# The deep stage's band mask: from TensorE's products to an addition on VectorE

## The reference

```
bq, bk2 = windows of 32 queries, each with the 64 keys of the window before and its own
mask = (it < jb) | (it > jb + w) | (jb == -1)
sim  = einsum('bhwie,bhwje->bhwij', bq, bk2) * 8
sim  = where(mask, -max, sim)
attn = softmax(sim, -1)
out  = einsum('bhwij,bhwje->bhwie', attn, bv2)
```

## Time and profile before

| | us |
|---|---|
| median of 3 runs | 4492.48 (4480.17 to 4496.16) |
| the profiled execution | 4489.61 |
| its span in the trace | 4487.9 |

### The profile page before, as it was taken

The page is one execution under the profiler, slowest core; times in us unless marked ns, Lnnn a source line. Parts: engine busy times, 40 slices in busy tenths (PEclk is TensorE's granted clock), DMA queues, the critical chain, the costliest instruction groups (busy, mean ns, idle before and its releaser), DMA issues.

```text
span 4487.9 us, 148433 instructions
## 1 busy us (share of the span) xinstructions
PE 4237.0 (94%) x66604; PEld 2403.9 (54%) x66604; DVE 3256.5 (73%) x4169; ACT 2676.0 (60%) x3161; POOL 2128.2 (47%) x1151
## 2 busy tenths in 40 slices
PE   7998899867999999999999996799999999999998
PEld 4544433434555555555555553455555555555554
DVE  6566666565877877877877866677877877877874
ACT  1451355323776776776776762466766766766764
POOL 0110000013665665666665650566666666666663
PEclk8998899978999999999999997899999999999999
DMA  2000000001111211121121111111211211121111
GB/s 84 1 2 1 0 1 1 1 0 35 33 33 29 58 33 54 33 58 30 33 58 29 33 33 50 24 31 31 58 32 31 58 32 55 33 57 30 33 33 29
DMA packets 78612, 144.88 MB, mean 32 GB/s; under 512 B 18648, under 2 KB 24992, under 8 KB 76448
## 3 DMA queue, kind: packets, MB, share of 16 engines
q1 hardware_dynamic: 77984, 135.39, 11.7%
HBM read 39.91 MB, written 1.05 MB: 9 GB/s over the span
## 4 chain that ended last, share of the span: by engine, by line
PE 77%; POOL 8%; issue 7%; DVE 6%; ACT 2%; DMA 0%; SPq 0%; POOLq 0%; DVEq 0%; ACTq 0%
PE psum L1307 13%; PE psum L1359 7%; PE psum L1332 6%; PE psum L1320 6%; PE psum L1276 5%; PE psum L667 5%; PE psum L1378 5%; PE psum L1290 4%; POOL arena L1739 3%; PE psum L1408 3%; PE psum L1424 3%; PE psum L1418 3%; PE psum L1373 3%; PE psum L699 3%; PE psum L721 3%
## 5 line engine op out<-in xcount | busy, mean ns | idle before, releaser
L1739 POOL TENSOR_TENSOR arena<-arena 128x1024 f32<-128x1024 f32 x384 | 722.3, 1902 | 881.8 <-ACT arena L1487 881.8
L1733 POOL TENSOR_TENSOR arena<-arena 128x1024 f32<-128x1024 f32 x384 | 907.5, 2363 | 245.0 <-DVE arena L1608 245.0
L1604 DVE TENSOR_TENSOR arena<-psum,arena 128x1024 f32<-128x1024 f32 x384 | 467.6, 1218 | 616.8 <-ACT arena L1480 616.6
L1480 ACT ACTIVATE arena<-psum 128x1024 f32<-128x1024 f32 x384 | 392.4, 1022 | 288.2 <-PE psum L1307 288.2
L1359 PEld LDWEIGHTS psum<-arena 64*64 64x64 f32 x24576 | 395.6, 135 | 211.8 <-issue 211.8
L1493 ACT ACTIVATE arena<-psum 128x1024 f32<-128x1024 f32 x384 | 390.8, 1018 | 194.6 <-PE psum L1320 194.6
L1608 DVE TENSOR_TENSOR arena<-psum,arena 128x1024 f32<-128x1024 f32 x384 | 466.4, 1215 | 0.0
L1615 DVE TENSOR_REDUCE h_pair<-arena 128x16 f32<-128x1024 f32 x384 | 464.2, 1209 | 0.0
L1359 PE MATMUL psum<-arena 64*64 64x32 f32 x24576 | 437.9, 221 | 5.2 <-DVE arena L1582 5.1
L1320 PE MATMUL psum<-w_ident,arena 128*128 128x128 f32 x3072 | 416.3, 279 | 23.5 <-POOL arena L1739 15.1
L1320 PEld LDWEIGHTS psum<-w_ident,arena 128*128 128x128 f32 x3072 | 338.2, 141 | 162.0 <-POOL arena L1739 94.6
(11 more groups left out here) (266 smaller groups left out, 7087.0 us busy)
## 6 DMA issues: line engine op xcount, KB each, us to landing
arena<-arena SPq DMA_DIRECT2D x672, 128.0 KB, 2.4
deep_wqkv<-in_deep_wqkv SPq DMA_DIRECT2D x6, 1536.0 KB, 7.2
arena<-in_deep_wqkv SPq DMA_DIRECT2D x6, 1536.0 KB, 7.1
arena<-arena SPq DMA_DIRECT2D x96, 64.0 KB, 2.0
deep_wo<-in_deep_wo SPq DMA_DIRECT2D x6, 512.0 KB, 7.5
arena<-in_deep_wo SPq DMA_DIRECT2D x6, 512.0 KB, 7.5
deep_w<-in_deep_w SPq DMA_DIRECT2D x6, 341.0 KB, 7.6
arena<-in_deep_w SPq DMA_DIRECT2D x6, 341.0 KB, 7.6
```

Source lines behind the costliest of these rows:

```text
L1480: nc.scalar.activation(qk_sq[:, HALVES[half], :], qk_half, ACT.Square).then_inc(de.deep_qk_squared, 1)
L1604: nc.vector.tensor_tensor(turned[:, hs, :].rearrange("p h (a e) -> p h a e", a=2), swapped, sin, ALU.mult).then_inc(de.deep_rope_parts, 1)
L1733: nc.gpsimd.tensor_tensor(roped[a % 2][:, hs, :], roped[a % 2][:, hs, :], turned[:, hs, :], ALU.add).then_inc(de.deep_summed, 1)
L1739: nc.gpsimd.tensor_tensor(roped[a % 2][:, hs, :], roped[a % 2][:, hs, :], over(h_inv[a % 2][:, hs], [P, LHEADS, LD]), ALU.mult).then_inc(d ...
```

## The change

The mask is no longer added on TensorE. The 8 mask products of each tile and their bfloat16 operands (`identb`, `maskb`) go, and each score product starts and stops by itself. A float mask `maskf` of 128 x 2 x 64 is kept in SBUF; for its first kind (the first tile of a sequence) only the 32 queries of the first window lack the keys before. `mask_dve` adds the mask to the scores out of PSUM and writes the sum into `probs`; the maximum is then taken from `probs`, and the subtraction reads and writes `probs`. The wait for the older transpose of `probs` moves from the subtraction to the addition. Where TensorE waited for `deep_less_max` to write the scores' banks again, it waits for `deep_masked`.

```diff
-        identb = sb("identb", [P, P], BF16)
-        maskb = sb("maskb", [P, 2, 2 * WIN], BF16)
+        maskf = sb("maskf", [P, 2, 2 * WIN])
...
             elif j == 1:
-                pe.wait_ge(de.deep_less_max, i)
-            for jj in range(WPT):
-                for r in range(2):
-                    r64, kind = slice(64 * r, 64 * r + 64), 1 if t or jj else 0
-                    mask = maskb[r64, kind, :].rearrange("p (o c) -> p o c", o=1).broadcast_to([64, PAIRS, 2 * WIN])
-                    nc.tensor.matmul(bank(r)[32 * jj:32 * jj + 32, :], identb[r64, 64 * r:64 * r + 32], mask, start=True,
-                                     stop=False, skip_group_check=True)
+                pe.wait_ge(de.deep_masked, i)
             scores_pe(j, 0)
...
-                                                kT[r64, pair, wi * WIN:(wi + 2) * WIN], start=False,
-                                                stop=(pair == PAIRS - 1), skip_group_check=True)
+                                                kT[r64, pair, wi * WIN:(wi + 2) * WIN], start=True, stop=True)
...
             if j + 1 < ALL:
-                pe.wait_ge(de.deep_less_max, i + 2)
+                pe.wait_ge(de.deep_masked, i + 2)
...
-        def max_dve(dve, c, j):
+        def mask_dve(dve, c, j):
             i = c * ALL + j
+            mask = maskf[:, 1 if j % TILES else 0, :].rearrange("p (o u c) -> p o u c", o=1, u=1).broadcast_to([P, PAIRS, 2, 2 * WIN])
             dve.wait_ge(de.deep_scores_ready, i + 1)
-            nc.vector.tensor_reduce(row_max, scores, AX.X, ALU.max).then_inc(de.deep_max, 1)
+            if j >= 2:
+                dve.wait_ge(de.deep_probs_turned, i - 1)
+            nc.vector.tensor_tensor(probs[j % 2], scores, mask, ALU.add).then_inc(de.deep_masked, 1)
 
         def less_max_dve(dve, c, j):
             i = c * ALL + j
+            dve.wait_ge(de.deep_masked, i + 1)
+            nc.vector.tensor_reduce(row_max, flat[j % 2], AX.X, ALU.max).then_inc(de.deep_max, 1)
             dve.wait_ge(de.deep_max, i + 1)
-            if j >= 2:
-                dve.wait_ge(de.deep_probs_turned, i - 1)
-            nc.vector.tensor_tensor(probs[j % 2], scores, row_max.rearrange("p (a r o) -> p a r o", r=2, o=1).broadcast_to(
-                [P, PAIRS, 2, 2 * WIN]), ALU.subtract).then_inc(de.deep_less_max, 1)
+            nc.vector.tensor_tensor(flat[j % 2], flat[j % 2], over(row_max, R), ALU.subtract).then_inc(de.deep_less_max, 1)
...
-                        nc.vector.tensor_copy(identb[:, :], w.ident[:, :]).then_inc(g.weights_scaled, 1)
-                        nc.vector.tensor_copy(maskb[:, :, :], raw["win_mask"]).then_inc(g.weights_scaled, 1)
+                        nc.vector.tensor_copy(maskf[:, :, :], raw["win_mask"]).then_inc(g.weights_scaled, 1)
...
-    first = band & (k >= WIN)
+    first = band & ((k >= WIN) | (p[:, None] >= WIN))
```

More of the change, by code:

```diff
@@ L1197, in program @@
                   "deep_sq_summed deep_clamped deep_sq_inv deep_inv_ready deep_rope_parts deep_summed deep_roped deep_turned deep_turn_kept "
-                  "deep_v_ready deep_v_kept deep_v_moved_0 deep_v_moved_1 deep_v_moved_2 deep_v_moved_3 deep_scores_ready deep_max deep_less_max deep_exped deep_row_sum deep_row_inv "
+                  "deep_v_ready deep_v_kept deep_v_moved_0 deep_v_moved_1 deep_v_moved_2 deep_v_moved_3 deep_scores_ready deep_masked deep_max deep_less_max deep_exped deep_row_sum deep_row_inv "
                   "deep_probs_ready deep_probs_turned deep_probs_kept deep_pv_done deep_o_kept deep_attn_ready "
@@ L1696, in deep_dve @@
                 if 0 <= s - 2 < ALL:
-                    max_dve(dve, c, s - 2)
+                    mask_dve(dve, c, s - 2)
                     less_max_dve(dve, c, s - 2)
@@ L1895, in _ @@
                         all_ready(pe)
-                        pe.wait_ge(g.weights_scaled, 5)
+                        pe.wait_ge(g.weights_scaled, 4)
                 elif kind == "chan":
```

## The result

The changed kernel takes 4672.85 us (median; 4665.07 to 4679.13) against 4489.19 for the one before: ratio 1.0402, 95% interval 1.0376 to 1.0428, 4% slower (the two medians alone give 1.0409). 4657 us was forecast. The profiled execution's span is 4676.3 us, 188.4 more than before.

The account below looks back on a forecast made before the run. TensorE is busy nearly without a gap, beside a scores-to-exponential chain with almost no slack. Steps sum to 3.43 us a unit, times 48 is 165 us: 4654.6, or 4657 us as median; range 4590 to 4735.

Parts of the forecast that it names:

- The chain and its slack of 0.3 us: Scores, maximum, subtraction, exponential, copy of turned q: 0.31 us slack before the second transposes in step 0, 0.32 in step 2.
- The collision, 0.35 us: New subtraction, two SBUF inputs, waits for GpSimd's second L1739 and ends 1.39 us later than now, against 1.04 never held up.
- Step 0: First of the four deep-stage steps in a unit (s mod 4): TensorE's L1290 waits for GpSimd's L1745, +1.48 us.
- 1 +1.05: Second step of a unit: L1408, waiting for the first gelu of L1536, moves from 2020.65 to 2021.70, +1.05 us.
- 2 +1.13: Third step of a unit: ScalarE's copy L1493 ends later, so TensorE's second L1320 starts at 2035.70 for 2034.57, +1.13 us.
- 3 -0.23: Fourth step of a unit: ten L1378 products hide the 1.39 us delay; TensorE keeps its 0.23 us gain.
- Mask products: Eight TensorE products leave each of 192 steps: 0.23 us a step, won only in step 3, about nothing in steps 0 to 2.
- The edges cancel: First steps of a call lose more (4 of them, some 1.4 us each), last units lose less; these 6 us cancel.
- VectorE's idle time (4481): Rival 1: VectorE's idle time swallows the added pass, leaving only step 3's 0.23 us gain: 4481 us, chance 0.06.
- the pass without the collision (4607): Rival 2: the pass is paid, the collision with GpSimd not; 2.38 us a unit, 114 us, 4607 us, chance 0.13.
- GpSimd first (4997): Rival 4: GpSimd goes first when L1739 ends, so the subtraction also waits for L1733's 2.36 us: 4997 us, chance 0.03.
- the third rival: TensorE's clock falls after step 0's gaps, once in each of 48 units: +82 us, 4739 us, chance 0.12.

Follow-up runs that it names:

- kernel with no mask: The kernel before with its 8 mask products taken out and no mask added, each score product starting and stopping by itself: 4483.24 us, ratio 0.9972.
- the kernel before with the early square root: The kernel before with ScalarE's square root put ahead of the squares of half 0 instead of behind them: 4483.37 us, ratio 0.9979.
- the two versions without maximum and subtraction: The changed kernel with the exponential directly after the mask addition: 4470.20 us; the same with ScalarE's square root ahead of the squares: 4401.15 us.
- the pass on the chain: The kernel before with a second maximum out of PSUM into a spare tile, waited for, between scores and maximum: 4659.38 us, ratio 1.0369.
- the subtraction from PSUM: The changed kernel with the subtraction reading the scores out of PSUM again, so only one input is in SBUF: 4640.06 us, ratio 1.0316.

## Why the prediction was right

- *The chain and its slack of 0.3 us.* Right. The gap ahead of the second transposes is 1.16 us in steps 0 and 2, named L1485, where 1.1 was forecast; counted from the start of the step they come 1.22 later, forecast 1.15 and 1.13. The pair of kernels with the same pass in and off the chain settles that place, not load, is the cause.
- *The collision, 0.35 us.* Right: the subtraction takes 1.57 us and ends 1.08 after GpSimd's instruction, forecast 1.57 and 1.08; without a second SBUF input both engines are back at their old durations.
- *Step 0 +1.48, 1 +1.05, 2 +1.13, 3 -0.23.* Measured +1.39, +1.06, +1.19, -0.14: 3.5 us a unit for 3.43, 168 us for 165. Step 0 was forecast 0.09 too long, steps 1, 2 and 3 too short by 0.01, 0.06 and 0.09, so that the unit comes within 0.07 partly because the misses offset each other. Step 3 kept 0.19 ahead of its second projections and lost 0.05 behind them.
- *Mask products: nothing in steps 0 to 2, 0.23 in step 3.* Right for the change and in the kernel with no mask; the reason was half right. I read 0.05 us of waiting for GpSimd (2066.84 to 2066.89); the kernel before with the early square root, whose steps 1 and 2 are 0.2 us shorter, shows that more hides there.
- *The edges cancel.* Too kind: the two calls together grew by 173.4 us (from the first projection to the last feed-forward product: 1664.8 and 1664.2 before, 1750.4 and 1752.0 after), 5 more than 48 units give.
- *The other 15.0 us of the span:* 14.5 lie ahead of the first deep call, which starts at 1079.7 us for 1065.2, in stages whose work is the same but for the copy of the mask. The granted clock over the multi-query stage was 0.91 in that execution, 0.95 in the one before. Over the twelve profiled executions that start lies between 1063.2 and 1079.7 us, and between 1065.7 and 1072.4 in the two versions without maximum and subtraction, which don't differ there, so it varies from execution to execution. The forecast's ratio, 4657 to 4492.48, is 1.0366, just under the measured interval; of the 16 us between 4657 and 4673, 9 are accounted for by the units and the edges (3.4 and 5.4), and the rest is left open.
- *Rivals.* VectorE's idle time (4481) fell by the pass on the chain, the pass without the collision (4607) by the subtraction from PSUM, GpSimd first (4997) by the row of the subtraction. The clock did not fall inside the steady steps of the changed kernel, where gaps stay at 1.16, so the third rival did not come true here. With the early square root on top, where the gap is 2.18, it came true in part, in 13 units of 44.

## What to carry to other kernels

Price an added pass by the slack of the chain in which it stands, step by step, and not by the engine's busy share: here the same pass cost 166 us or nothing. Removing work from the bounding engine is worth only what the next wait lets through; look for that wait first, since moving one square root (37 and 69 us by the medians, once the two passes were gone) was worth more than taking the mask products out alone (9 us). And where an operation is moved from PSUM to SBUF, look at what GpSimd does at that moment.

## What the runs showed of the hardware

- A VectorE instruction with two SBUF inputs and a GpSimd tensor_tensor on SBUF do not work at once, by the times of their ends. Whichever comes second waits for the other's end, and the wait stands in its recorded duration: VectorE 0.36 us on average, GpSimd 1.0 us (2.36 to 3.35). "SBUF — State Buffer" of the Trainium skill, section "Who interferes with whom", says so, and the traces agree. With PSUM as one of the two inputs there was no such wait (1224 ns), nor for the maximum, which has one input, in SBUF (1220 ns with L1733 running beside it).
- A maximum over 1024 elements took 1220 ns from SBUF and 1225 from PSUM. The 62 cycles' difference that the Trainium skill gives in "VectorE: DVE Perf Modes", in the section on the TRN2 errata, did not appear.
- TensorE's granted clock fell to its lower level after 13 of 44 gaps of about 2.2 us that are alike in their rows, and after two of six stops of 0.7 to 2.7 us. It never fell after the changed kernel's steady gaps of 1.16 us, two to a unit. So a gap of 2.2 us can cost the clock here and mostly did not.
- A recorded gap of TensorE can be shorter than the wait: groups with nothing to wait for start 0.14 us before the recorded end of the one before (L1312 behind L1383), so a gap of 0.26 us was a wait of 0.40.
